# A selective-scan kernel: diagonals of B built by DMA, two copies moved from VectorE to ScalarE, carries in pairs

## The reference

```python
delta = jax.nn.softplus(delta + delta_bias[None, :, None])
def step(h, inp):
    ut, dt, bt, ct = inp
    dA = jnp.exp(dt[..., None] * A4)
    h = dA * h + (dt * ut)[..., None] * bt[:, :, None, :]
    y = jnp.einsum('bkdn,bkn->bkd', h, ct)
    return (h, y)
...
y = out_y[:, 0] + inv_y[:, 0] + wh_y + invwh_y
```

## Time and profile before

| | us |
|---|---|
| median of 3 runs (6708.61 to 6716.85) | 6715.05 |
| profiled execution | 6713.79 |
| its span, first to last instruction | 6712.1 |

### The profile page before, as it was taken

One profiled execution on the slowest core, in us unless ns is written; L12 is line 12 of the kernel. 1 busy time (PEld: TensorE's weight loads), 2 busy tenths in 40 slices (PEclk: granted clock), 3 DMA queues, 4 the chain that ended last, 5 costly groups with the idle time before them and its releaser, 6 DMA issues. The chain is left out here.

```text
span 6712.1 us, 130278 instructions
## 1 busy us (share of the span) xinstructions
PE 5830.3 (87%) x41691; PEld 5150.7 (77%) x41691; DVE 4764.7 (71%) x6882; ACT 3496.8 (52%) x7658; POOL 2798.1 (42%) x2159
## 2 busy tenths in 40 slices
PE   7789889898887998888888544999999989999998
PEld 6688778887766887888877333888888878888887
DVE  2799999999818999999997554555556556555554
ACT  2799999999737999999997211111111111111110
POOL 0688888888716888888887000000000000000000
PEclk8899999999988999999999877999999989999999
DMA  2122222222221222222222115666666667666665
GB/s 68 68 88 89 83 83 89 88 89 83 90 70 71 88 89 83 87 85 88 90 83 98 32 47 143 153 149 139 142 148 152 155 149 157 144 140 142 150 151 143
DMA packets 552406, 719.16 MB, mean 107 GB/s; under 512 B 37814, under 2 KB 458518, under 8 KB 518038
## 3 DMA queue, kind: packets, MB, share of 16 engines
q1 hardware_dynamic: 551382, 705.17, 38.6%
q10 hardware_dynamic: 720, 10.49, 0.4%
HBM read 677.22 MB, written 38.31 MB: 107 GB/s over the span
## 5 line engine op out<-in xcount | busy, mean ns | idle before, releaser
L663 POOL TENSOR_TENSOR read<-state,c_wide 128x1024 f32<-128x1024 f32 x1024 | 2435.0, 2378 | 459.2 <-DVE state L719 455.8
L719 DVE TENSOR_TENSOR_SCAN state<-decay,carry,p_drive 128x512 f32<-128x512 f32 x1792 | 2145.7, 1259 | 10.1 <-POOL carry L666 5.3
L617 ACT ACTIVATE decay<-step,a_neg 128x512 f32<-128x512 f32 x2048 | 1416.2, 714 | 230.2 <-DVE state L719 229.9
L1614 PE MATMUL p_y<-window,x_high 128*128 128x256 f32 x7936 | 1506.5, 288 | 0.0
L1677 ACT COPY term_blocks<-p_s 128x256 f32<-128x256 f32 x832 | 310.4, 373 | 2195.0 <-PE p_s L1614 2195.0
L1614 PEld LDWEIGHTS p_y<-window,x_high 128*128 128x128 f32 x7936 | 1253.9, 193 | 0.0
L510 PE MATMUL p_drive<-diag_b,xu_tok 128*128 128x128 f32 x8192 | 1101.3, 285 | 119.8 <-DVE state L719 116.1
L510 PEld LDWEIGHTS p_drive<-diag_b,xu_tok 128*128 128x128 f32 x8192 | 1007.8, 196 | 212.8 <-DVE state L719 151.2
L1614 PE MATMUL p_y<-window,x_low 128*128 128x256 f32 x3968 | 1138.8, 287 | 0.0
L521 PE MATMUL p_y<-ident,read 128*128 128x128 f32 x8192 | 1078.2, 275 | 3.8 <-POOL read L663 3.8
L521 PEld LDWEIGHTS p_y<-ident,read 128*128 128x128 f32 x8192 | 942.2, 143 | 4.7 <-POOL read L663 4.7
(11 more groups left out here) (245 smaller groups left out, 5822.3 us busy)
## 6 DMA issues: line engine op xcount, KB each, us to landing
c_wide<-c_scratch SPq DMA_DIRECT2D x256, 1024.0 KB, 4.6
window<-taps_scratch SPq DMA_DIRECT2D x448, 257.0 KB, 6.2
window<-taps_scratch SPq DMA_DIRECT2D x768, 129.0 KB, 4.6
window<-taps_scratch SPq DMA_DIRECT2D x192, 513.0 KB, 7.2
window<-taps_scratch SPq DMA_DIRECT2D x64, 385.0 KB, 5.9
gate_scratch<-gate_out SPq DMA_DIRECT2D x16, 512.0 KB, 3.1
gate_in<-gate_scratch SPq DMA_DIRECT2D x8, 1024.0 KB, 6.4
mix_weights<-in_M_plus SPq DMA_DIRECT2D x32, 256.0 KB, 7.2
```

What stands on the lines that cost most here:

```text
L617: act.activation(decay[:, n % 2, t, :], step[:, c.parity, t, :], ACT.Exp, scale=m.a_neg[:, DT2 * c.k + t, n:n + 1]).then_inc(s["decay"], 1)
L663: pool.tensor_tensor(read[:, n % 4, :, :], state[:, n % 4, :, :], wide, ALU.mult).then_inc(s["read_out"], 1)
L719: dve.tensor_tensor_scan(flip(state[:, n % 4, t, :], c), flip(decay[:, n % 2, t, :], c), flip(p_drive[:, n % 2, t, :], c), 0.0 if c.start ...
L1614: last = pe.matmul(out, x[:, source, blk, :], view[:, :, at:at + P][:, :, ::-1], start=first and x is m.x_high and z == 0, stop=True, skip ...
```

## The change

- The diagonals for odd states are no longer made by ACT. SP writes the eight odd rows of B by single values into the diagonals of a DRAM scratch (8 states x 4 blocks of 128 x 128, zero elsewhere), and reads them back as matrices of two states each, into a tile with two places. The scratch has two parities and is zeroed once at the start.
- The stores of C and B for the next chunk are issued earlier, ahead of the C load for states 8 to 11; the wait for their landing stands before the next chunk's first loads. The semaphore `c_ready` goes.
- `keep_x` and `keep_y` move from DVE to ACT: `keep_x` behind the decays at n = 10 and 11, `keep_y` behind those at n = 3.
- POOL copies two states' carries at once, after each odd state. The scan of state n then waits for n // 2 - 1 pairs.

```diff
+            sp.wait_ge(idmade, 4)
+            for parity in range(2):
+                sp.dma_start(m.diag_dram[parity].rearrange("(r x) -> r x", r=P), blank[:, :]).then_inc(m.w_stored, 16)
...
+            pool.memset(blank[:, :], 0.0).then_inc(idmade, 1)
...
-            sp.wait_ge(m.w_stored, 16)
+            sp.wait_ge(m.w_stored, 48)
...
-        diag = sb("diag_b", [P, NB4, P])
+        diag = sb("diag_b", [P, 2, 2, NB4, P])
...
-            def store_c(c):
+            def store_rows(c):
                 sp.wait_ge(s["xd_kept"], START + c.g + 1)
                 sp.dma_start(m.c_dram[c.parity], xd[C_ROW:C_ROW + NS, :]).then_inc(s["c_stored"], 16)
-                sp.wait_ge(s["c_stored"], START + c.g * 16 + 16)
-                sp.sem_inc(s["c_ready"], 1)
+                image = m.diag_dram[c.parity]
+                diagonals = bass.AP(tensor=image.tensor, offset=image.offset,
+                                    ap=[[NB4 * P * P, ODD], [P * P, NB4], [P + 1, P]])
+                rows = xd[B_ROW + 1:B_ROW + NS:2, :].rearrange("n (i p) -> n i p", p=P)
+                with nc.allow_non_contiguous_dma(reason="one value to each place of a diagonal"):
+                    sp.dma_start(diagonals, rows).then_inc(s["c_stored"], 16)
+
+            def load_diag(c, d):
+                if not (c.first and d < 2):
+                    sp.wait_ge(s["driven"], START + c.q * 2 + (8 * d - 8))
+                at = 2 * d * NB4 * P * P
+                src = m.diag_dram[c.parity, at:at + 2 * NB4 * P * P].rearrange("(n p q) -> p n q", n=2 * NB4, p=P)
+                sp.dma_start(diag[:, d % 2, :, :, :].rearrange("p n i q -> p (n i) q"), src).then_inc(
+                    s[f"diag_in{d % 2}"], 16)
...
             def body(c, nxt):
                 if c.first:
-                    store_c(c)
+                    store_rows(c)
+                    sp.wait_ge(s["c_stored"], START + c.g * 32 + 32)
+                    load_diag(c, 0)
                     widen_c(c, 0)
+                    load_diag(c, 1)
                     widen_c(c, 1)
+                load_diag(c, 2)
+                if nxt:
+                    store_rows(nxt)
                 widen_c(c, 2)
+                load_diag(c, 3)
                 widen_c(c, 3)
                 if nxt:
-                    store_c(nxt)
+                    sp.wait_ge(s["c_stored"], START + nxt.g * 32 + 32)
+                    load_diag(nxt, 0)
                     widen_c(nxt, 0)
+                    load_diag(nxt, 1)
                     widen_c(nxt, 1)
...
             def drive(c, n):
-                pe.wait_ge(s["scaled"], START + c.q + (n + 1))
+                if n % 2 == 0:
+                    pe.wait_ge(s["scaled"], START + c.g * ODD + (n // 2 + 1))
+                elif n % 4 == 1:
+                    pe.wait_ge(s[f"diag_in{n // 4 % 2}"], START + c.g * 32 + (16 * (n // 8) + 16))
...
-                    if of:
+                    if of and at % 2 == 0:
                         times_b(of, at)
                     of, at = following(c, nxt, n + 2)
                     if of:
                         decays(of, at, 1)
+                    if n == 3 and not c.first:
+                        keep_y(Before(c))
                     if nxt and n in preparation:
                         preparation[n](nxt)
+                    if nxt and n in (10, 11):
+                        keep_x(nxt, n - 10)
...
-                pool.tensor_copy(carry[:, n, :], state[:, n % 4, :, end]).then_inc(s["carried"], 1)
+                if n % 2:
+                    pool.tensor_copy(carry[:, n - 1:n + 1, :], state[:, n % 4 - 1:n % 4 + 1, :, end]).then_inc(s["carried"], 1)
...
-                        dve.wait_ge(s["carried"], START + c.q + (n - 3))
+                        dve.wait_ge(s["carried"], START + c.g * ODD + (n // 2 - 1))
```

More of the change, by code:

```diff
@@ L24 @@
 NCH = T // L
+NB4 = L // P
+ODD = NS // 2
 START = 16
@@ L63, in constants @@
         w_conv = sb("w_conv", [P, 2, DT2, 9, P], fp32r)
+        blank = sb("blank", [P, ODD * NB4 * P])
         ps = [ctx.enter_context(nc.psum_tensor(f"wps{i}", [P, 512], fp32)) for i in range(8)]
@@ L353 @@
 SCAN_SEMAPHORES = [
-    "projected", "xd_kept", "c_stored", "c_ready", "c_in0", "c_in1", "b_turned", "b_kept", "step_mm", "step_max",
+    "projected", "xd_kept", "c_stored", "c_in0", "c_in1", "diag_in0", "diag_in1", "b_turned", "b_kept", "step_mm", "step_max",
     "step_abs", "step_exp", "step_ln", "step", "step_u", "x_turned", "x_kept", "scaled", "driven", "decay", "scanned", "carried",
@@ L399, in scans @@
         ps = lambda n, sh: ctx.enter_context(nc.psum_tensor(n, sh, fp32))
-        NB4 = L // P
         xd = sb("xd", [P, L])
@@ L509, in drive @@
                         else:
-                            last = pe.matmul(o, xu_tok[:, c.parity, i, t * P:t * P + P], diag[:, i, :], start=True,
-                                             stop=True)
+                            last = pe.matmul(o, xu_tok[:, c.parity, i, t * P:t * P + P],
+                                             diag[:, n // 4 % 2, n // 2 % 2, i, :], start=True, stop=True)
                     last.then_inc(s["driven"], 1)
@@ L580, in keep_projection @@
                 act.wait_ge(s["b_turned"], START + c.g)
-                act.wait_ge(s["c_stored"], START + c.g * 16)
+                act.wait_ge(s["c_stored"], START + c.g * 32)
                 act.copy(xd[:, :], p_prep[:, :]).then_inc(s["xd_kept"], 1)
@@ L606, in times_b @@
                 for i in range(NB4):
-                    dst, src = ((scaled[:, i, :], xu_tok[:, c.parity, i, :]) if n % 2 == 0 else
-                                (diag[:, i, :], m.ident[:, :]))
-                    last = act.activation(dst, src, ACT.Copy, scale=b_tok[:, c.parity, i, n:n + 1])
+                    last = act.activation(scaled[:, i, :], xu_tok[:, c.parity, i, :], ACT.Copy,
+                                          scale=b_tok[:, c.parity, i, n:n + 1])
                 last.then_inc(s["scaled"], 1)
@@ L618, in decays, with keep_x, keep_y @@
                                scale=m.a_neg[:, DT2 * c.k + t, n:n + 1]).then_inc(s["decay"], 1)
+            def keep_x(c, half):
+                act.wait_ge(s["x_turned"], START + c.g * 2 + (half + 1))
+                if not c.first:
+                    act.wait_ge(s["scaled"], START + c.g * ODD + -ODD)
+                    act.wait_ge(s["driven"], START + c.q * 2 + -2 * NS)
+                act.copy(xu_tok[:, c.parity, 2 * half:2 * half + 2, :],
+                         p_prep[:, :].rearrange("p (i d) -> p i d", d=DI)).then_inc(s["x_kept"], 1)
+            def keep_y(c):
+                act.wait_ge(s["summed"], START + c.q + NS)
+                act.wait_ge(s["y_turned"], START + c.g * 2)
+                act.copy(y_tok[:, :, :], p_y[:, :, :]).then_inc(s["y_kept"], 1)
             act.preload_act_table_set("natural_log_exp_and_others")
@@ L628, in body @@
                     step_ln(c)
-                    for n in range(2):
-                        times_b(c, n)
+                    keep_x(c, 0)
+                    keep_x(c, 1)
+                    times_b(c, 0)
                     for n in range(2):
@@ L644, in body @@
                         decays(of, at, 1)
+                    if n == 3 and not c.first:
+                        keep_y(Before(c))
                     if nxt and n in preparation:
                         preparation[n](nxt)
+                    if nxt and n in (10, 11):
+                        keep_x(nxt, n - 10)
+                if c.last:
+                    keep_y(c)
             chunk_stream(act, b, body)
@@ L702, in finish_step @@
                                   ALU.add).then_inc(s["step"], 1)
[L704 to L710, removed]
             def scan(c, n, t):
@@ L721, in scan @@
                                        ALU.mult, ALU.add).then_inc(s["scanned"], 1)
[L723 to L726, removed]
             def add_y(c, t):
@@ L747, in body @@
                     begin_y(1)
-                    keep_x(c, 0)
-                    keep_x(c, 1)
                 for n in range(NS):
                     scan(c, n, 0)
-                    if n == 3 and not c.first:
-                        keep_y(Before(c))
                     if n in (6, 7) and not c.first:
@@ L759, in body @@
                         finish_step(nxt)
-                    if nxt and n in (11, 12):
-                        keep_x(nxt, n - 11)
                     scan(c, n, 1)
                 if c.last:
-                    keep_y(c)
                     add_y(c, 0)
@@ L1887, in program @@
         m.t2_dram = nc.dram_tensor("attended_scratch", [NB, T, C], fp32, kind="Internal").ap()
+        m.diag_dram = nc.dram_tensor("diag_scratch", [2, ODD * NB4 * P * P], fp32, kind="Internal").ap()
         m.c_dram = nc.dram_tensor("c_scratch", [2, NS, L], fp32, kind="Internal").ap()
```

## The result

The changed kernel takes 6554.26 us (median of 4 runs, 6549.5 to 6559.76) against 6714.93 for the kernel before; the ratio is 0.9759, its 95% interval 0.9743 to 0.9774. That is 161 us less, where 211 were forecast: the right sign and inside the range, 50 us above the point. The profiled execution has a span of 6547.8 us.

What follows compares the result with a forecast made beforehand. VectorE's queue plus its waits for PE and ACT was taken as the bound; 4.5 - 0.5 - 0.7 = 3.3 us a chunk over 64 chunks gives 211 us, so 6504 us on the median's scale, range 6425 to 6690.

Steps and rivals of the forecast that it cites:

- What bounds the kernel: Scan stage: VectorE's own queue, plus its waits for PE and ACT, makes the chunk of 49.5 us.
- Copies leave DVE: Per chunk, 2.34 us of copy work and the copies' waits leave VectorE, 4.5 us in all.
- The wait in finish_step: VectorE's wait of 1.39 us a chunk stays, as step_ln is still issued behind the same ACT work.
- keep_y on ACT: At state 3, the y copy delays decays of state 6 by 1.1 us, within slack; PE's wait costs nothing.
- Carries in pairs: POOL in the run of scans: even states need a later read, charged as 0.5 us a chunk lost.
- PE nearly tight: PE from state 8's scan to the next step product: 0.5 us late, plus 0.2 for the clock, 0.7 a chunk.
- falls of the clock: PE's lowered granted clock loses 0.5 us a chunk, of which 0.2 was taken to reach VectorE.
- sum of the new stalls: Carries in pairs 0.5 and PE 0.7, together 1.2 us a chunk taken off the gain.
- rival (b): PE and POOL pace the chunk: stalls of 2.5 us a chunk, gain 2.0, 6585 us; chance 0.19.
- The diagonals by DMA: SP's queue: scattered store of 4096 single values takes 4.7 us on eight engines, hidden, loads cost nothing.
- Rival (a): The scattered store is too slow, 33 us, and delays the C load: 7565 us; chance 0.18, including 40 to 64 ns.
- The signs of being wrong: Read waiting for c_wide, PE's drive for diag_b, 4-byte packets over 33 ns, or VectorE waiting over 2 us a chunk.

Runs made afterwards that it cites:

- e2: The changed kernel with both copies back on VectorE and single carries, so diagonals by DMA alone: 6731.56 us, ratio 1.0035 to the kernel before.
- e1: The kernel before with only both copies moved to ScalarE, diagonals still made by ScalarE and single carries: 6727.17 us, ratio 1.0025.
- e10: The changed kernel with single carries, the first step product one y sum earlier, and 24 of 128 transposes a chunk left out: 6448.37 us, ratio 0.9614.
- e9: The changed kernel with half of the y sums of states 8 to 13 left out (24 of 128 transposes a chunk): 6495.44 us, ratio 0.9687.
- e3: The changed kernel with a carry copy after each state, as before, instead of pairs: 6549.97 us, ratio 0.977 to the kernel before.
- e4: The changed kernel with the next chunk's first step product issued one y sum earlier on PE: 6542.54 us, ratio 0.9759 to the kernel before.
- e7: The changed kernel with the scattered store issued twice, the second time into another scratch: 6548.82 us, ratio 0.9765 to the kernel before.
- e8: The changed kernel with the scattered store issued four times: 7268.54 us, ratio 1.0831 to the kernel before.
- e12: The changed kernel with the scattered store issued three times: 6858.76 us, ratio 1.0227 to the kernel before.
- e5: The changed kernel with keep_x back on VectorE, keep_y staying on ScalarE: 6594.21 us, ratio 0.9822 to the kernel before.

## Why the prediction was right, point by point

**What bounds the kernel.** Right that ACT alone does not: e2 takes 9.4 us of work a chunk from ACT and gains nothing. But DVE's queue is not the bound by itself either: e1 takes 4.5 us from it, and the chunk stays. Behind it ACT, and what waits for ACT, stands at the same length.

**Copies leave DVE, 4.5 us a chunk.** Right in size, as far as shown: e10, with both ties loosened and 24 transposes fewer on PE, is 4.3 us under before. The sum that it comes from is 0.4 loose: 46.5 of work and 2.03 + 1.39 of waits are 49.9, not 49.5; the chunk of the earlier trace rows is 50.1 long, a little over the mean. But the text priced this part as if it stood by itself. It does not: e1 has it alone and is slower than before. What makes it a gain is the room on ACT, of which the prediction said only that ACT "loses its backlog and I cost it at nothing".

**The wait in finish_step stays at 1.39.** Right: 27.4 / 21 = 1.30 us a chunk.

**keep_y on ACT holds nobody up.** Right in the changed kernel (no wait of PE for y_tok stands among its larger ones); in e1 it held PE for 1.4 us a chunk.

**Carries in pairs, 0.5 us.** The wait before state 12 was forecast at 0.2 to 0.3 and measured at 0.40; all carry waits are 12.0 / 21 = 0.6 a chunk. Left out was the spacing of the scans: 17 of them at 1.20 instead of 1.18 are 0.4 us that no wait names, and e9 and e10 give about 0.8 to both. A pair on POOL is 4.80 us, not 4.77.

**PE nearly tight, 0.7 us.** The wait in step_bias was forecast at 0.5 and measured at 0.60 in the chunk shown, 14.2 / 21 = 0.7 in the mean; waits for drives add 0.2. The 0.2 for the falls of the clock can't be told apart in this: the granted clock of the stretch is 0.98, against 0.99 before. The mechanism was right, but the prediction added the two stalls as if each stood alone: PE is the first tie, and it stays when the carries are freed (e3) or the product is moved (e4).

**The term that was mis-sized** is thus the sum of the new stalls, put at 1.2 us a chunk. Measured it is 4.5 - 2.6 = 1.9: carries 0.6, scans held to their pace 0.4, PE 0.7 + 0.2. The parts are read off one stretch and do not close better than some 0.3: two pauses of 3.7 and 2.6 us in it are another 0.3 a chunk. The 0.7 missing are 42 us over the 60 steady spacings. Another 16 are missing because the prediction gave all 64 chunks the full gain, and the four others, at the start of each image, have none. Against these 58 stand some 11 us outside of the scans, nearly all in the unchanged part behind them, so that the profiled span is only 47 short of the forecast and the median 50. For the prediction these 11 are luck. The case was between the forecast and rival (b), which had 2.5.

**The diagonals by DMA.** The store was taken at 4.7 us, by 9.1 ns on eight engines; it holds SP's queue 6.2 us (e7, e8). That 4.7 is so near is luck, as two errors work against each other. The eight engines, which the prediction took from the page it names, are not borne out: e8 shows some sixteen at work, which with 9.1 ns would make 2.3 us. And a value is busy for 19.8 ns (e8), not 9.1. The deadline was put at 17 us after its issue and is 6.2 + 7 = 13. Both errors are on the bad side and neither reached the result. Rival (a) is real as a mechanism: two more stores make the kernel slower than before (e12). In the trace the store's stretch, 884 to 890 us, has

```profile
DMA packets 4293, 0.60 MB, mean 100 GB/s; under 512 B 3249, under 2 KB 4273, under 8 KB 4289
...
q1 hardware_dynamic: 4293, 0.60, 81.6%
```

that is 0.816 x 16 x 6 us / 4293 = 18 ns a packet, of which three quarters are single values: as in e8 twice the 9.1 of the small loads, far from the 64 of the earlier trace rows. The rule of the Trainium skill ("DMA: Bandwidth & Descriptors", Specifications), that a write below 512 B is read, modified and written, is compatible with the doubling, but no run here writes the same number of longer pieces, so that the reason for it stays open. Costing the loads at nothing was wrong by up to 0.28 us a chunk (e2). In the changed kernel two such pauses, of 3.7 and 2.6 us, stand between 700 and 1700 us.

**The signs of being wrong.** None came: no read waits for c_wide and no drive for diag_b from 700 to 1700 us, a value takes under 33 ns, and DVE waits 1.6 us a chunk for PE and POOL, under the 2 named, though the slow scans make it just 2.0.

## What to carry to other kernels

Where four engines are each busy for some 90% of a loop, ask whether the engine that receives work must be relieved in the same edit: here each half alone lost about 20 us, and both together gained 160. After the sum for the engine that sets the pace, go through the longest run in which it used to pause, and count every other engine's work in that run; a pause that goes was also the others' time to come up, and here half of what it cost was all there was to gain (e5). A transfer that is hidden deserves its slack in us beside its price: here doubling it cost nothing and tripling it more than the whole change brought. And where the time of two stretches is compared, look first at how much of the difference lies in code that was not changed.

## What the runs showed of the hardware

4096 single values of 4 B, written from SBUF to places 516 B apart in DRAM, take 6.2 us, 1.5 ns each over all DMA engines (e7, e8). Alone on the queue they keep 87% of the sixteen engines busy, 19.8 ns a packet, though the outermost dimension is eight (e8). They keep whatever stands behind them on SP's queue waiting: behind four such stores the issue of a C load took 6.04 us instead of 0.33. An ACT copy of 128x1024 from PSUM took 0.99 us and of 128x512 0.58, DVE's 1.23 and 0.67.
